# The first of seven attentions computed image by image, its band applied along the free axis, and the short attentions one group later

## The reference, cut to what matters

```
x   = patches @ W + b + positions                     # tokens
# stage 1, attention with a band over neighbouring tokens, residual without projection
y   = LN(x) * g + c;  q, k, v = split(y @ Wqkv.T + bias)
kb  = k[t-1] + k[t] + k[t+1]   (within the image),  qb likewise
s   = (1.2 * q . k  -  0.2 * qb . kb) / sqrt(16);  x = LN(x + softmax(s) v)
held = x;  h = LN(x)                                  # a norm of a norm
# stage 2, causal attention on h, projection, residual;  stage 3, experts with a capacity
# stage 4, attention without its own token, projection:  x = LN(2 x + y + b);  held = x;  h = RMS(x)
# stages 5 to 12: four attentions with 64 channels a head, each with a dense or an expert layer behind it
```

## Time and profile before

| what | us |
|---|---|
| median of the runs | 1997.62 |
| the profiled execution's own time | 1996.22 |
| its span | 1994.4 |
| stage 1 ends (first score matmul of stage 2 starts) | 243.6 |
| stage 2: to the last group's projection | 371.5 |
| stage 3: first expert matmul starts | 399.3 |
| stage 4: first score matmul starts, first projection of stage 5 starts | 526.3, 650.4 |

### The profile page before, as it was taken

One profiled execution on the slowest core, in us unless ns is written; L12 is line 12 of the kernel. 1 busy time (PEld: TensorE's weight loads), 2 busy tenths in 40 slices (PEclk: granted clock), 3 DMA queues, 4 the chain that ended last, 5 costly groups with the idle time before them and its releaser, 6 DMA issues.

```text
span 1994.4 us, 34415 instructions
## 1 busy us (share of the span) xinstructions
PE 1696.3 (85%) x12228; PEld 1568.7 (79%) x12228; DVE 1080.5 (54%) x3055; ACT 768.6 (39%) x1833; POOL 591.8 (30%) x1369
## 2 busy tenths in 40 slices
PE   7999999697588899899988999688989999788970
PEld 6999877497377798788877888678878888788960
DVE  2454446533465577656774334357765777443427
ACT  1232243142243455445442544244543544244420
POOL 3355424400675321351222000444226122300030
PEclk7799577599566899999988999879989998899985
DMA  4030001144009600100002565400011000156530
GB/s 125 21 104 17 0 1 35 49 148 153 21 20 283 205 1 2 60 17 1 15 15 88 184 201 194 151 17 1 1 45 33 1 15 15 54 179 207 196 93 25
DMA packets 77118, 149.39 MB, mean 75 GB/s; under 512 B 6312, under 2 KB 56594, under 8 KB 76853
## 3 DMA queue, kind: packets, MB, share of 16 engines
q1 hardware_dynamic: 70614, 134.92, 21.2%
q0 software_dynamic: 6336, 12.26, 2.2%
HBM read 107.10 MB, written 41.05 MB: 74 GB/s over the span
## 4 chain that ended last, share of the span: by engine, by line
PE 53%; issue 17%; DVE 16%; POOL 5%; DMA 5%; ACT 3%; SPq 1%; another core or an unknown queue 0%; DVEq 0%; POOLq 0%; ACTq 0%
PE ps_proj L1119 9%; PE ps_proj L1228 5%; PE ps_proj L1133 4%; PE ps_score L1299 4%; PE ps_pt L1093 4%; PE ps_o L1200 4%; PE ps_proj L1045 3%; DMA w_in<-w_all_dram 3%; PE ps_proj L1282 3%; PE ps_score L1167 2%; PE ps_score L1157 2%; PE ps_score L1066 2%; PE ps_o L1190 2%; PE ps_o L1080 1%; DVE prob L1591 1%
## 5 line engine op out<-in xcount | busy, mean ns | idle before, releaser
L1299 PE MATMUL ps_score<-w,hid 128*112 128x192 f32 (+2 forms) x1680 | 305.1, 334 | 9.4 <-DVE x L1905 5.5
L1299 PEld LDWEIGHTS ps_score<-w,hid 128*112 128x112 f32 (+2 forms) x1680 | 277.3, 180 | 11.8 <-DVE x L1905 7.3
L1482 POOL TENSOR_SCALAR tmp<-rs,var 111x1 f32<-111x1 f32 x154 | 54.5, 354 | 703.0 <-DVE rs L1562 702.4
L1421 ACT ACTIVATE hid<-ps_proj 128x224 f32<-128x224 f32 (+2 forms) x360 | 133.5, 382 | 265.9 <-PE ps_proj L1282 252.3
L1470 POOL DMA_INDIRECT tin<-rows_out,idx x66 | 68.2, 1033 | 492.4 <-issue 383.1
L1093 PE MATMUL ps_pt<-const,prob 111*111 111x111 f32 x748 | 142.1, 306 | 43.3 <-ACT probt L1409 22.5
L1409 ACT ACTIVATE probt<-ps_pt 111x333 f32<-111x333 f32 x220 | 98.4, 447 | 182.6 <-PE ps_pt L1093 182.0
L1093 PEld LDWEIGHTS ps_pt<-const,prob 111*111 111x111 f32 x748 | 107.3, 199 | 66.7 <-issue 28.5
L1228 PE MATMUL ps_proj<-wo,ot 128*111 128x192 f32 (+1 forms) x616 | 137.0, 371 | 7.7 <-ACT ot L1387 7.1
L1401 ACT ACTIVATE prob<-prob 111x333 f32<-111x333 f32 (+1 forms) x242 | 117.4, 487 | 61.4 <-DVE prob L1591 51.3
L1200 PEld LDWEIGHTS ps_o<-v,probt 111*111 111x111 f32 x1056 | 127.3, 193 | 0.5
(11 more groups left out here) (253 smaller groups left out, 4285.2 us busy)
## 6 DMA issues: line engine op xcount, KB each, us to landing
w_in<-w_all_dram SPq DMA_DIRECT2D x64, 768.0 KB
w<-w_all_dram SPq DMA_DIRECT2D x50, 576.0 KB, 5.2
rows_in<-zero SPq DMA_DIRECT2D x1, 12320.0 KB, 49.5
rows_out<-zero SPq DMA_DIRECT2D x1, 9240.0 KB, 83.1
tin<-rows_in SPq DMA_DIRECT2D x36, 224.0 KB
rows_out<-tout SPq DMA_DIRECT2D x36, 168.0 KB
patch<-patches_dram SPq DMA_DIRECT2D x11, 333.0 KB, 2.9
wo<-wo_all_dram SPq DMA_DIRECT2D x6, 576.0 KB, 3.9
```

The costliest lines, as they stand in the source:

```text
L1299: last = pe.matmul(bank[0:n, 0:C], hid[:, i % 2, m, at:at + n], w2[:, slot, m, :], start=(m == 0), stop=(m == FC - 1))
L1421: act.activation(hid[:, i % 2, m, 0:n], bank[:, 0:n], ACT.Relu if b.tile is None else ACT.Gelu).then_inc(taken, 1)
```

## The change

Stage 1 becomes a short attention. Its scores are taken by image in two products: q scaled by 1.2/4 with k, and the banded q scaled by -0.2/4 with the banded k. The band is now two additions along the free axis on VectorE for a block of three groups (step BD), the scaling into three head columns is ScalarE's (step QS). No mask matmul is left in stage 1. The output `o` is brought back to a token per partition by three DMAs of 37 partitions each (`spread_out`), and the step XA adds it to x. The gain and bias of the first norm are applied on VectorE (step NX), the value bias by a matmul of one row. `neigh_lead` puts four of the eleven TOK steps ahead of the first projection. The first weights come by the same rounded path as all others (load 0), and patches, expert weights and the first zero fill are issued from within the list.

In all three short stages PT, PV, OT, Y stand later: S(n), then OT(n-2), PT(n-1), Y(n-2), E(n), PV(n-1), V(n+1).

The norm of a norm is one root on two columns: since the first norm has mean 0 and a known variance, both roots are taken from the same statistics (`TWICE`), and the step N2 is gone.

```diff
+def neigh_lead():
+    return [("TOK", 0), ("TOK", 1), ("W1", LOAD0[("att", NEIGH)]), ("TOK", 2), ("NX", 0), ("A", 0), ("TOK", 3), ("NX", 1),
+            ("A", 1), ("NX", 2), ("A", 2), ("QK", 0, 0), ("QK", 0, 1), ("TOK", 4), ("BD", 0, 0), ("QK", 0, 2),
+            ("QK", 0, 3), ("QS", 0, 0, 0), ("QS", 0, 0, 1), ("BD", 0, 1), ("NX", 3), ("V", 0, 0), ("QS", 0, 1, 0),
+            ("TOK", 5), ("QS", 0, 1, 1), ("NX", 4)]
+NEIGH_QS = {(1, 2): [(0, 0)], (2, 0): [(0, 1)], (2, 1): [(1, 0)], (2, 2): [(1, 1)]}
-LOGITS_AHEAD = {0: 8, 2: len(LOGIT_AT), 4: len(LOGIT_AT)}
-COUNTS_AHEAD = {0: 7, 2: len(COUNT_AT), 4: len(COUNT_AT)}
+LOGITS_AHEAD = {0: 9, 2: len(LOGIT_AT), 4: len(LOGIT_AT)}
+COUNTS_AHEAD = {0: 8, 2: len(COUNT_AT), 4: len(COUNT_AT)}
...
 def short_order(a, last_stage, follower):
-    for n in range(G + 1):
+    for n in range(G + 2):
         slots = short_fill(a, n, last_stage, follower)
         if n < G:
             out.append(("S", n, 0))
         out += slots[0]
-        if n:
-            out.append(("PV", n - 1, 1))
+        if n >= 2 and a != NEIGH:
+            out.append(("OT", n - 2, 0))
+        if 1 <= n <= G:
+            out.append(("PT", n - 1, 0))
+        if n >= 2:
+            out.append(("XA", n - 2) if a == NEIGH else ("Y", n - 2))
+        out += slots[1]
         if n < G:
             out.append(("E", n, 0))
-        out += slots[1]
-        if n < G:
-            out.append(("PT", n, 0))
-        if n:
-            out.append(("OT", n - 1, 0))
+        if 1 <= n <= G:
+            out.append(("PV", n - 1, 1))
         out += slots[2]
-        if n:
-            out.append(("Y", n - 1))
-        out += slots[3]
-    if a == DIAG:
-        out += [("N2", g) for g in range(G) if ("N2", g) not in out]
...
+TWICE = {("att", NEIGH): ("XA", LN_EPS), ("att", DIAG): ("Y", RMS_EPS)}
...
+            def spread_out(g):
+                if g >= 2:
+                    sp.wait_ge(stats_ready, NORMS[(("att", NEIGH), "XA", g - 2)] + 1)
+                sp.wait_ge(o_ready, OUT_AT[(NEIGH, g, 1)] + 1)
+                for i in range(IPG):
+                    sp.dma_start(o_small[i * NTOK:(i + 1) * NTOK, g % 2, :],
+                                 o[0:NTOK, g % 2, i * C:(i + 1) * C]).then_inc(small_in[g % 2], 16)
...
+                        parts = [(short_q(b % 2), short_k(b % 2))]
+                        if a == NEIGH:
+                            parts.append((qband[:, b % 2, :, :, :, :], neigh_kb(b % 2)))
                         for j in range(2):
                             for i in range(IPG):
-                                for e, bank in enumerate(banks):
...
+                                for part, (q_t, k_t) in enumerate(parts):
+                                    for e, bank in enumerate(banks):
...
+            def by_head(dst, rows_of, b, j, which):
+                src = rows_of.rearrange("p (g t) -> p g t", t=TP)[:, :, 0:TG].rearrange("p g (i q) -> p g i q", i=IPG)
+                for h in range(3):
+                    ins = act.activation(dst[:, j, 0:BLOCKS[b][1], :, h * NTOK:(h + 1) * NTOK], src, ACT.Copy,
+                                         scale=scales[:, which, j, h:h + 1])
...
+                if twice:
+                    link(pool.tensor_tensor(z, r, r, ALU.mult))
...
+                    link(pool.tensor_tensor(r, u, t, ALU.mult))
+                    link(centred(xng, xg, rs[:, m, 1:2]))
+                    link(pool.tensor_copy(xn[0:TG, g, C:CX], xn[0:TG, g, 128:C]))
+                    link(centred(xg, xg))
+                    pool.tensor_copy(held[:, g, :], xg).then_inc(norm_done, 1)
+                    return
...
+            def band(b, which):
...
+                link(dve.tensor_copy(dst[:, :, :, 0:1], src[:, :, :, 0:1]))
+                link(dve.tensor_tensor(dst[:, :, :, 1:], src[:, :, :, 1:], src[:, :, :, 0:end], ALU.add))
+                tell(dve.tensor_tensor(dst[:, :, :, 0:end], dst[:, :, :, 0:end], src[:, :, :, 1:], ALU.add), band_done,
+                     2 * b + which + 1)
...
+                elif kind == "XA":
+                    g = step[1]
+                    dve.wait_ge(small_in[g % 2], 16 * IPG * (g // 2 + 1))
+                    norm_slot(key)
+                    link(dve.tensor_tensor(x[:, g, :], o_small[:, g % 2, :], x[:, g, :], ALU.add))
+                    start_norm(key, x[:, g, :], False, LN_EPS, TWICE[st][1])
...
-                elif kind == "N2":
```

More of the change, by code:

```diff
@@ L62, in __init__ @@
         self.t5 = a >= T5
-        self.short = a in (CAUSAL, DIAG)
+        self.short = not self.t5
         self.d = T5_D if self.t5 else SMALL_D
[L65 to L68, removed]
+        self.chunks = H // 2 if self.t5 else 2
         self.proj = a != NEIGH
-        self.pe_mask = not self.t5
         self.qk = 2 * self.chunks
@@ L163 @@
 FFN = {f: ffn_blocks(f) for f in range(LAYERS + 1)}
-def qkv(a, g):
-    return [(kind, g, j) for kind in ("Q", "K", "V") for j in range(ATTS[a].items)]
 def first_block(a):
     s = ATTS[a]
[L173 to L202, removed]
-        if n < units:
-            steps.append(("S", g, u))
-        if 1 <= n <= units:
-            steps.append(("E", (n - 1) // 4, (n - 1) % 4))
-        if 2 <= n < units + 2:
-            steps.append(("PT", (n - 2) // 4, (n - 2) % 4))
-        if 3 <= n:
-            steps.append(("PV", (n - 3) // 4, (n - 3) % 4))
-        for x in steps:
-            out.append(x)
-            if x[0] == "E":
-                continue
-            gap += 1
-            upto = min(-(-count * gap // 12), count)
-            out += fill[given:upto]
-            given = max(given, upto)
-        if u == 3:
-            out += fill[given:]
-            given = count
-    out += fill[given:]
-    out += [("N2", g) for g in range(G) if ("N2", g) not in out]
-    return out
@@ L549 @@
 PROJ, SCORE, TURNED, READY, NORMS = numbered()
-SPLIT = [key for key in TURNED if key[0] != ("att", NEIGH)]
+SPLIT = list(TURNED)
 def att_load(a, step):
@@ L1102, in att_step @@
                     turn(st, g)
+                elif kind == "TOK":
+                    bank = proj_bank(key)
+                    pe.wait_ge(patch_in[g % PATCH_RING], 16 * (g // PATCH_RING + 1))
+                    for c in range(PCH):
+                        last = pe.matmul(bank[0:TG, 0:C], patch[:, g % PATCH_RING, c, :], tokw[:, c, :],
+                                         start=(c == 0), stop=(c == PCH - 1))
+                    last.then_inc(proj_full, 1)
                 elif kind == "QK":
@@ L1134, in att_step @@
                                          w[:, slot, c, at:at + s.vwide], start=(i == 0),
-                                         stop=(i == len(terms) - 1))
+                                         stop=(i == len(terms) - 1 and a != NEIGH))
+                    if a == NEIGH:
+                        last = pe.matmul(bank[0:TG, 0:C], const[0:1, K_ONES:K_ONES + TG], early[0:1, Y_VB:Y_VB + C],
+                                         start=False, stop=True)
                     last.then_inc(proj_full, 1)
```

531 lines of the change are left out of this document (232 added, 299 removed).

## The result

The changed kernel takes 1925.89 us in the median (1922.94 to 1929.32, 4 runs), against 1994.98 us for the kernel before, measured beside it: a ratio of 0.966 (95% interval 0.9631 to 0.9688). The profiled execution took 1929.32 us, with a span of 1927.5. The forecast was 1917, with a range of 1872 to 1962. In what follows the differences are between spans: 1994.4 - 1927.5 = 66.9 us less, where 79.1 were forecast. (Medians are of all executions and ratios of the undisturbed ones alone, and since both profiles of the kernel with the order alone, e2_order_only and r_e2, caught disturbed executions, only its ratios are used further down.)

The account below looks back on a forecast made before the run. TensorE's work and its clock were taken as the bound. Savings of 54.6 (stage 1), 8 (stage 2), 2.5 (behind it), 10 (stage 4) and 4 (start of stage 5) made 79.1, from 1996.2 to 1917 us; range 1872 to 1962.

Parts of the forecast that it names:

- First score at 54: Stage 1: the first score matmul starts at 54 us, after the lead of tokens, norms, projections, bands and scalings; 45 to 62.
- TensorE's work 122.9 us: Stage 1 from its first score: work left, 156.9 us at 1.2 GHz, takes 122.9 at stage 2's clock of 0.66.
- The list at 2.4 GHz: Stage 1's remaining TensorE work priced at full clock: 84.1 us in all, against 156.9 at 1.2 GHz.
- The first two rivals: Stages 1, 2 and 4: cold throughout at 1.2 GHz, 2016 us, chance 0.08; warm throughout at 2.4 GHz, 1809, chance 0.06.
- together 12: Stage 1's waits: 8 us at three block changes, 4 for late setup and second weight split ahead of a division; 4 to 25.
- 5 to 8 us: Stage 1: V, next scores and shift between a division and its XA hide the spread's three issues and 2.9 us.
- sign of being wrong: Stage 1's spread: XA among the long waits on a DMA of `o_small` would show the prediction wrong.
- I take 8 of them as gone: Stage 2: of TensorE's 9.4 us of waits the later order removes 8; bounds 0 and 9.4.
- What is late next there is TensorE's own work.: Stage 2: with 8 of 9.4 us of waits gone, TensorE's own work is what sets the time next.
- 9.8 of 10: Stage 4: of TensorE's 19.1 us of waits 10 go; bounds 0 and 17.
- its 4 us behind the stage: Start of stage 5: with N2 gone, 4 us of TensorE's 5.3 us wait for the first shift go; 0 to 5.3.
- The fourth rival: Stages 2 and 4: later order gives nothing, TensorE at 1.2 GHz being the bound; 1935 us; chance 0.72 together with the forecast.

Follow-up runs that it names:

- e2_order_only: The kernel before with only the later order in stages 2 and 4; stage 1 and the separate norms as before: ratio 0.9822.
- r_e2: The kernel before with only the later order in stages 2 and 4, profiled a second time: ratio 0.9916.
- e1_tail: The changed kernel with XA(9) one place later and XA(10) moved into stage 2, behind its second group's shift: 1916.31 us, ratio 0.955.
- e4_no_spread: The changed kernel without the 33 spread DMAs, so the first attention's output is not added: 1912.13 us, ratio 0.9549.
- e3_old_order: The changed kernel with the old order in stages 2 and 4; new stage 1 and joined norm stay: 1931.46 us, ratio 0.9644.
- e7_joined_only: The kernel before with only stage 4's two norms joined in one root: 1983.21 us beside 1985.67, ratio 0.9977.
- r_after: The changed kernel, unaltered, profiled once more: 1910.74 us beside 1985.67 for the kernel before, ratio 0.9628.
- e5_comb: The changed kernel with only stage 4's first combination and its gather put ahead of the first scores: 1915.2 us, ratio 0.9641.
- b1_all: The changed kernel with XA(9) and XA(10) later, scalings ahead of V's copies, stage 4's first combination ahead of the first scores: 1898.49 us, ratio 0.9564.
- r_b1: The kernel with three moves (XA(9) and XA(10), scalings, stage 4's first combination) profiled once more: 1901.47 us, ratio 0.9589.
- b2_late: The kernel with three moves (last XAs, scalings, first combination), its late setup moved from group 3's round to group 8's: 1890.12 us, ratio 0.9544.
- e8_stall_back: The kernel with three moves (last XAs, scalings, first combination) with the XA(9) and XA(10) move undone: 1905.43 us, ratio 0.9586.

## Why the prediction was right, and where it was not

**Stage 1's work: right.** First score at 54, measured 52.6; TensorE's work 122.9 us, measured 123.3 (119.1 in the second profile). Building the stage from the work that is left, at prices of stage 2's rows, was sound, and so was its clock of 0.66 (0.67 and 0.70). (The list at 2.4 GHz has two halves wrong: half of 10.2 is 5.1 and not 5.6, half of 5.1 is 2.6 and not 2.8. With them the stage comes to 122.4 us.) The first two rivals fall with it: stages 1, 2 and 4 ran neither at 1.2 GHz throughout nor at 2.4.

**Stage 1's waits: mis-sized.** The term "together 12" measured 19.4. The block changes were 7.9 of the 8 forecast; the 4 us left for everything else on VectorE and ScalarE measured 11.5: value products that waited for the copy of the turned probabilities (4.3), projections and turns behind splits and token norms (2.7, 2.7 and 0.9), and the rest in shorter pieces. TensorE was busy for 86% of the stretch, where over 90 was named as the sign of being right.

**The spread: right inside the stage, missed at its end.** The prediction counted "5 to 8 us" of other work between the division of group n-2 and XA(n-2), and took nothing. That holds while there are groups to come: VectorE waited for the spread in only three of eleven groups, 2.2 us at XA(2), 5.8 at XA(9) and 6.5 at XA(10). The last two are where no next scores and no shift are left to stand between, and the last reaches TensorE. So a sign of being wrong that the prediction had named, XA waiting long on a DMA of `o_small`, did show, at the joint alone. The rows give what a spread takes: issue from 196.51 to 198.28, data used at 202.91, 6.4 us in all, where three issues (1.8) and 2.9 would have made 4.7.

**Stage 2: this step failed.** "I take 8 of them as gone", and "What is late next there is TensorE's own work." What was late next was VectorE, held by stage 1's last XA: waits of 18.5 us. And without that stall they are not 1.4 but 10.3 (e1_tail) or 8.6 (e4_no_spread): the waits for exponentials, divisions and output copies that the order aimed at did shrink, from 5.9 us before to 1.5 in e1_tail, and turns that wait for splits (1.3 before, 6.6) took their place. So the order's worth doesn't lie in fewer waits there. With the stall, the old order in e3_old_order waited 15.1 us and the new one 16.9 to 18.5, and the old one is longer by 3.5 to 8.7 us all the same, because TensorE was busy for 121.3 us at 0.63 and not for 109.2 to 115.9 at 0.64 to 0.69. No step of the prediction had this, and one profile of the old order doesn't show that the order causes it.

**Behind stage 2, and stage 4.** 1.6 of 2.5 us, and eight scatters stand behind the last norm, as forecast. In stage 4 9.8 of 10, but not by the path foreseen: TensorE's waits fell by 5.2 us (19.7 to 14.5), its busy time by 4.6. The waits that the order aims at nearly went, from 13.7 us to 1.2; others grew, the turns of the combined rows from 2.7 to 7.7 in all and the waits for splits and for V's copies from 0.3 to 3.8. The joined norm hides as forecast, and its 4 us behind the stage measured 4.2 by itself (e7_joined_only) and 2.8 in the kernel after.

**The sum.** 48.3 - 0.3 + 1.6 + 9.8 = 59.4 us up to T5's first score and 2.8 of the wait behind it make 62.2 that belong to the change, where 79.1 were forecast. The other 4.7 us, 0.7 in stage 3 and 4.0 in the rest, lie within what unchanged stages scatter over; that they filled part of the gap is luck. The size of stage 1's part hangs on the execution as well: beside e7_joined_only, which has the old stage 1 and ran on the same chip in the same batch, r_after ends stage 1 at 192.1 and not 246.6, 54.5 us earlier, where 54.6 were forecast, and takes 4.1 us more in stage 2. The fourth rival (1935: no gain in stages 2 and 4) describes stage 2 in the numbers, but not in its reason, since TensorE wasn't the bound there; stage 4 it has wrong.

## What to carry to other kernels

When a transfer is hidden by the next iteration's work, look at the last iteration: there the consumer stands directly behind the transfer, and on an in-order engine the next stage's first steps queue behind it. Move the last consumers into the next stage. And when a stage runs at a mean clock well below 1.0, a closed wait of w us is worth anything from nothing to more than w: read busy time and clock together, compare profiles in which the clock rose at the same point of the work, and time the whole kernel before believing the stage.

## What was unexpected of the hardware

One order of work can meet several clocks. Stages 1 and 2 are the same code in the kernel after, its repeat and e5_comb, and stage 2 was busy for 109.2, 113.1 and 115.9 us, at 0.69, 0.66 and 0.64. Yet it can repeat to 0.02 us: 102.69 us at 0.76 in b1_all, r_b1 and b2_late, and 115.9 at 0.64 in both e5_comb and e8_stall_back. All these stages hold the same 917 matmul records in the same order. What goes with the outcome is how long before the stage's first score the clock had last risen. The 4 us ahead of that score, in the kernel after, its repeat, e5_comb and b1_all:

```profile
191.33:195.33 4.00, 3.88 (x39) 3.62 (x37) 1.62 (x7) 2.14 (x6) 0.19 (x1) 0.85 0.03 10
188.10:192.10 4.00, 3.87 (x42) 3.28 (x40) 1.01 (x4) 2.84 (x8) 0.69 (x2) 0.96 0.04 13
187.10:191.10 4.00, 3.87 (x40) 3.62 (x40) 1.38 (x6) 2.42 (x7) 0.00 (x0) 0.89 0.03 11
185.21:189.21 4.00, 3.86 (x39) 3.62 (x39) 2.09 (x6) 2.36 (x6) 0.00 (x0) 0.88 0.03 11
```

A mean of 0.85 over 4 us is 2.8 us at 2.4 GHz behind 1.2 at 1.2 GHz; 0.96 is 3.7 us, 0.88 and 0.89 are 3.1 (e4_no_spread has 0.86, e1_tail 0.97). Sorted by that time, stage 2's length (and TensorE's busy time) in us:

| clock risen before the first score | with the stall | without it |
|---|---|---|
| 2.8 or 2.9 | 127.6 (109.2), after | 120.8 (112.2), e4_no_spread |
| 3.7 | 130.3 (113.1), after again | 123.3 (113.0), e1_tail |
| 3.1 | 132.8 (115.9), e5_comb and e8_stall_back | 114.3 (102.7), b1_all, its repeat and b2_late |

So in one row the stall costs 6.8, 7.1 or 18.5 us, and down one column the same order differs by up to 9. That may be why the medians of e8_stall_back and b1_all hardly differ: each execution can meet another row. It is not shown, since no run moved this time alone, and what sets it isn't known.

The windows of 10 us late in stage 2 of e8_stall_back:

```profile
276.40:286.40 10.00, 10.00 (x62) 8.64 (x61) 4.07 (x16) 3.30 (x11) 4.76 (x10) 0.50 0.07 23
286.40:296.40 10.00, 10.00 (x75) 8.75 (x75) 6.55 (x27) 1.76 (x6) 4.20 (x9) 0.50 0.08 24
296.40:306.40 10.00, 10.00 (x76) 8.57 (x75) 5.84 (x25) 2.94 (x9) 3.83 (x9) 0.50 0.08 24
```

and of r_b1:

```profile
258.10:268.10 10.00, 9.57 (x83) 8.39 (x83) 4.40 (x18) 4.02 (x12) 3.51 (x9) 0.73 0.07 22
268.10:278.10 10.00, 9.85 (x106) 7.96 (x105) 8.19 (x36) 4.60 (x14) 4.88 (x10) 1.00 0.08 24
```

Busy for 10.00 of 10 us, three stretches in a row, TensorE stayed at 1.2 GHz; busy 9.57 and then 9.85, it went from a mean of 0.73 to 1.00, 2.4 GHz. The Trainium skill, "TensorE: Matmul & The Clock Gate", section "Why this matters for your kernels", advises to keep TensorE busy without gaps to get and hold the full clock; the first three rows disagree with it for this mix of thin products. Why the two kernels part here isn't settled by these runs.
